# Layer 2 of a four-layer graph network by two tanh and a mask applied afterwards, and residual sums split over two engines

## What is computed

```
e     = leaky(einsum('bid,bjd->bij', x * a0, x))     # slope 0.2
alpha = sigmoid(where(adj == 1, e, -3.4e38))         # 0 where there is no edge
out   = alpha @ x + bias
```

## Time and profile before

| | us |
|---|---|
| median of 3 runs | 270.03 (268.92 to 270.17) |
| span of the profiled execution, first to last instruction | 268.6 |
| VectorE busy in it | 247.2 (92%) |
| TensorE busy (matmul) | 237.0 (88%) |
| ScalarE busy | 217.9 (81%) |
| GpSimd busy | 139.0 (52%) |

### The profile page before, as it was taken

How to read it: one execution, slowest core, us unless ns; L and a number is a source line. 1 busy time by engine, 2 the same in 40 slices (tenths; PEclk the granted TensorE clock), 3 DMA queues, 4 the chain that set the end, 5 groups by cost and what they waited for, 6 DMA issues and landing times.

```text
span 268.6 us, 6069 instructions
## 1 busy us (share of the span) xinstructions
PE 237.0 (88%) x1825; PEld 210.1 (78%) x1825; DVE 247.2 (92%) x956; ACT 217.9 (81%) x626; POOL 139.0 (52%) x161
## 2 busy tenths in 40 slices
PE   7887969889998999999999899999999959996850
PEld 7765768678886989888898788988999859785740
DVE  1598998999999989999999999999999999999883
ACT  1366525688899999899899999999999979977841
POOL 1001102511384485689647717554598457778851
PEclk9999988999999999999999999999999999999985
DMA  6597371000070003506000633103000110100033
GB/s 237 193 307 264 118 248 67 1 2 0 2 263 13 2 0 115 202 14 221 1 5 0 198 114 122 41 1 121 0 2 0 41 41 7 36 0 1 4 117 122
DMA packets 12147, 21.79 MB, mean 81 GB/s; under 512 B 1104, under 2 KB 5968, under 8 KB 12112
## 3 DMA queue, kind: packets, MB, share of 16 engines
q1 hardware_dynamic: 11680, 21.17, 22.9%
q10 hardware_dynamic: 432, 0.20, 0.3%
HBM read 17.17 MB, written 4.19 MB: 80 GB/s over the span
## 4 chain that ended last, share of the span: by engine, by line
DVE 49%; PE 28%; issue 8%; POOL 6%; ACT 5%; DMA 2%; DVEq 0%; POOLq 0%; ACTq 0%
PE banks L1123 13%; DVE wgt_all L808 10%; DVE fstats L856 8%; DVE fres L849 7%; DVE fres L841 5%; POOL frstd L542 4%; DVE wgt_all L815 3%; PE banks L1089 3%; DVE raw_all L731 3%; PE banks L1064 2%; PE banks L1120 2%; PE banks L1133 2%; DMA adj_all<-adj_turned 2%; PE banks L1081 1%; PE banks L1049 1%
## 5 line engine op out<-in xcount | busy, mean ns | idle before, releaser
L542 POOL TENSOR_TENSOR frstd<-fvar,minus_half 128x4 f32<-128x4 f32 x64 | 74.2, 1165 | 104.7 <-DVE fvar L862 36.6
L1123 PE MATMUL banks<-vals_all,wgt_all 128*128 128x129 f32 x512 | 64.4, 279 | 3.1 <-DVE wgt_all L808 2.9
L1123 PEld LDWEIGHTS banks<-vals_all,wgt_all 128*128 128x128 f32 x512 | 60.6, 194 | 4.8 <-issue 3.2
L808 DVE SCALAR_TENSOR_TENSOR wgt_all<-banks,gain,maskT 128x256 f32<-128x256 f32 x128 | 52.6, 473 | 0.6 <-PE banks L1081 0.3
L538 POOL TENSOR_TENSOR xb<-xs_all,bias_cen 128x256 f32<-128x256 f32 x60 | 44.1, 760 | 8.6 <-DVE xs_all L765 4.4
L856 DVE BATCH_NORM_STATS2 fstats<-fres 128x6 f32<-128x256 f32 x128 | 47.8, 416 | 0.0
L1089 PE MATMUL banks<-fxT,fxTa 128*128 128x256 f32 x128 | 35.8, 382 | 0.0
L1123 PE MATMUL banks<-xs_all,wgt_all 128*128 128x128 f32 x256 | 31.6, 277 | 4.8 <-DVE wgt_all L815 4.7
L1123 PEld LDWEIGHTS banks<-xs_all,wgt_all 128*128 128x128 f32 x256 | 29.9, 192 | 5.4 <-issue 3.2
L640 ACT ACTIVATE xs_all<-fres,frstd 128x128 f32<-128x128 f32 x96 | 30.9, 425 | 1.9 <-POOL frstd L542 1.8
L578 ACT COPY fxT<-banks 128x256 f32<-128x256 f32 x64 | 21.1, 396 | 10.9 <-PE banks L1049 10.8
(11 more groups left out here) (95 smaller groups left out, 463.1 us busy)
## 6 DMA issues: line engine op xcount, KB each, us to landing
adj_all<-adj_turned SPq DMA_DIRECT2D x16, 512.0 KB, 4.8
xT_all<-x_turned SPq DMA_DIRECT2D x16, 256.0 KB, 4.7
x_all<-x_laid SPq DMA_DIRECT2D x16, 256.0 KB, 4.4
out<-xs_all SPq DMA_DIRECT2D x16, 256.0 KB, 2.4
bias<-biases_laid SPq DMA_DIRECT2D x1, 128.0 KB, 3.6
w_pack<-W_and_columns ACTq DMA_DIRECT2D x1, 68.0 KB, 2.6
w_fast<-W_turned ACTq DMA_DIRECT2D x1, 64.0 KB, 4.1
w_nat<-in_L_gnn_W ACTq DMA_DIRECT2D x1, 64.0 KB, 4.4
```

Of the source, the lines that this page charges most:

```text
L542: nc.gpsimd.tensor_tensor(frstd[:, int(l), slot(n), :], fvar[:, int(l), slot(n), :], minus_half[:, :, :], ALU.pow).then_inc(fast_pool[k], 1)
L808: last = nc.vector.scalar_tensor_tensor(out=wgt(u)[:, c, :], in0=place(f"rows{l}", u), scalar=gain[:, u, c, 1:2], in1=maskT(u)[:, c, :], o ...
L1123: last = nc.tensor.matmul(place(f"out{l}", u)[:, b * width:(b + 1) * width], wgt(u)[:, c, b * P:(b + 1) * P], (vals if l in "01" else xs)( ...
```

## The change

1. `score` has no second product: L1090, `minus_big`, `raw` and its ring go. ScalarE takes `Tanh` of half the score and of a tenth of it; VectorE takes the larger as before (now called `umax`, into `sg`), and a new second pass (`alpha`) makes (tanh + 1) times the mask. The mask holds 0.5 instead of 1, so that this is the sigmoid. Layer 3's weights are doubled once to make up for it (one VectorE instruction), and `seen` reads the masks.
2. `res2` of teams 0 to 13 and `res3` of teams 0 to 10 become two steps: `lift`, a ScalarE copy from PSUM to `fres`, and a GpSimd addition in SBUF. Teams 14 and 15 of `res2` and 11 to 15 of `res3` stay on VectorE.
3. Small steps change engine: `var` of 16 team-layers and one `fscale` go from VectorE to GpSimd; `norm2` is on ScalarE for all 16 teams (5 were on VectorE), `norm3` for 15 (13), `norm1` for 14 (16); one `mask` and one `high` go to VectorE, and VectorE has two `bias2` and two `bias3` where it had two `bias3`.
4. All five orders and the bank table are new. Rings: `ADJ` 4 (3), `MASK` 10 (9), `SG` 4 (3), `RAW` gone. In SP's order the loads of teams 12 to 15 are now interleaved with the stores of teams 0 to 4.

The diff, cut to its core:

```
-X_IN, XT_IN, ADJ, RAW, MASK, XS, FXT, FXTA, VALS, WGT, SG, FRES, XB = 4, 3, 3, 7, 9, 6, 7, 5, 6, 7, 3, 9, 5
+X_IN, XT_IN, ADJ, MASK, XS, FXT, FXTA, VALS, WGT, SG, FRES, XB = 4, 3, 4, 10, 6, 7, 5, 6, 7, 4, 9, 5
+EDGE = 0.5
...
# order of ScalarE, end
+        "sigmoid:15 norm2:13 high:13 agg:12 norm3:11 agg:13 norm2:14 high:14 norm2:15 high:15 agg:14 norm3:12 agg:15 "
+        "norm3:13 norm3:14 norm3:15"
...
# order of VectorE, end
+        "bias2:14 norm1:15 bias2:15 res3:11 stats3:11 stats2:13 var3:11 var2:13 norm3:10 umax:14 alpha:14 umax:15 "
+        "alpha:15 res2:14 stats2:14 var2:14 res2:15 stats2:15 var2:15 res3:12 stats3:12 res3:13 stats3:13 var3:12 "
+        "var3:13 bias3:15 low:15 res3:14 stats3:14 res3:15 stats3:15 var3:15"
...
# GpSimd
+            def residual(l, n, k):
+                for u in graphs(n):
+                    biaser = doer(f"bias{l}", n)
+                    pool.wait_ge(signals[biaser][k], at(biaser, f"bias{l}", u))
+                    pool.wait_ge(fast_act[k], at("act", f"lift{l}", u))
+                    nc.gpsimd.tensor_tensor(fres(u)[:, :, :], fres(u)[:, :, :], xb(u)[:, :, :], ALU.add).then_inc(fast_pool[k], 1)
+            def variances(l, n, k):
+                pool.wait_ge(fast_dve[k], at("dve", f"stats{l}", final(n)))
...
+                nc.gpsimd.tensor_scalar(var, squares, factor, floor, ALU.mult, ALU.add).then_inc(fast_pool[k], 1)
...
# ScalarE
-                    nc.scalar.copy(maskT(u)[:, :, :], adj_in(u)[:, :, :]).then_inc(fast_act[k], 1)
+                    nc.scalar.activation(maskT(u)[:, :, :], adj_in(u)[:, :, :], ACT.Copy, scale=EDGE).then_inc(fast_act[k], 1)
...
-                    nc.scalar.activation(sg(u), scored, ACT.Sigmoid)
-                    nc.scalar.activation(wgt(u), scored, ACT.Sigmoid, scale=SLOPE).then_inc(fast_act[k], 1)
+                    nc.scalar.activation(sg(u), scored, ACT.Tanh, scale=0.5)
+                    nc.scalar.activation(wgt(u), scored, ACT.Tanh, scale=0.5 * SLOPE).then_inc(fast_act[k], 1)
+            def lift(l, n, k):
+                act.wait_ge(fast_pe[k], at("pe", f"out{l}", final(n)))
+                for u in graphs(n):
+                    nc.scalar.copy(fres(u)[:, :, :], place(f"out{l}", u).rearrange("p (b c) -> p b c", b=NB)).then_inc(fast_act[k], 1)
...
# VectorE
-                    nc.vector.tensor_scalar(raw(u), adj_in(u)[:, :, :], -1.0, 1.0, ALU.mult, ALU.add).then_inc(fast_dve[k], 1)
...
+            def larger(l, n, k):
+                for u in graphs(n):
+                    dve.wait_ge(fast_act[k], at("act", "sigmoid", u))
+                    nc.vector.tensor_tensor(sg(u), sg(u), wgt(u), ALU.max).then_inc(fast_dve[k], 1)
             def alpha(l, n, k):
-                    nc.vector.tensor_tensor(wgt(u), sg(u), wgt(u), ALU.max).then_inc(fast_dve[k], 1)
+                    nc.vector.scalar_tensor_tensor(out=wgt(u), in0=sg(u), scalar=1.0, in1=maskT(u), op0=ALU.add, op1=ALU.mult).then_inc(fast_dve[k], 1)
...
# TensorE
-                        nc.tensor.matmul(place("score", u)[:, c * N:(c + 1) * N], fxTa(u)[:, c * P:(c + 1) * P], fxT(u)[:, :], start=True, stop=False)
-                        last = nc.tensor.matmul(place("score", u)[:, c * N:(c + 1) * N], minus_big[:, :], raw(u)[:, c, :], start=False, stop=True)
+                        last = nc.tensor.matmul(place("score", u)[:, c * N:(c + 1) * N], fxTa(u)[:, c * P:(c + 1) * P], fxT(u)[:, :], start=True, stop=True)
...
+            def emptied_by(phase, n):
+                lifted = doer(f"res{phase[-1]}", n) == "pool"
+                return (fast_act, "act", f"lift{phase[-1]}") if lifted else (fast_dve, "dve", f"res{phase[-1]}")
```

114 lines of the change are left out of this document (69 added, 45 removed), and 196 rows, old and new, of tables (BANKS, ORDER).

## The result

The changed kernel takes 282.61 us, the median of 4 runs (279.82 to 284.27), and the kernel before 270.10 in 4 runs beside it; the ratio is 1.043, with a 95% interval of 1.034 to 1.053. Some executions of a kernel are over 1.5% slower than its fastest; ratios and intervals in this document leave them out, medians and ranges keep them. The changed kernel is slower by 12.5 us where the forecast had it faster by 5.

What follows compares the result with a forecast made beforehand. VectorE was taken as the bound, with ScalarE and TensorE also full in the middle. Span 268.6 - 8.8 - 2.5 + 3.5 + 2.6 = 263.4 us, plus 1.4 gives 264.8 us; range 258 to 271.5.

Steps and rivals of the forecast that it cites:

- the work counted out: VectorE's instructions removed, moved and added, summed part by part: -8.8 us, between -10.7 and -4.9.
- the term of the shared resource: GpSimd's additions and VectorE passes slow each other by waiting: +3.5 us, bounds 0 and 26.
- GpSimd's queue: On GpSimd, `pow` queues behind additions that wait for their lifts, delaying `norm` and `center1`; costed at nothing.
- The price of the new pass: VectorE's new `alpha` pass in layer 2: 0.66 us each, +21.1 us, bounds +19.2 and +25.0.
- 10.6 us for `raw`: VectorE's `raw` passes go, 0.66 us a team over 16 teams: -10.6 us.
- 16.5 for the sums: 25 residual sums leave VectorE, 0.66 us each: -16.5 us.
- the ends: Start and end of the kernel; the last team's `norm2` and `norm3` move to ScalarE: +2.6 us, bounds 0 and +5.
- TensorE's relief: 64 products, 17.4 us busy, leave TensorE; half of VectorE's idle time between 20 and 201 us credited: -2.5 us.
- Rival 4: ScalarE's table loads stay, so its middle work grows: 281.8 us, chance 0.04.
- rival 2: ScalarE becomes the bound of the middle through lifts and normalizations: 269.5 us, chance 0.13.
- rival 3: The saving comes whole; additions meet nothing new and moved normalizations hide: 258.7 us, chance 0.18.
- Rival 1: The lock between VectorE passes with two SBUF inputs and GpSimd additions costs more than gained: 273.4 us, chance 0.13.

Runs made afterwards that it cites:

- e8: The changed kernel without layer 2's new second VectorE pass (mask and +1 left out): 265.4 us, ratio 0.986.
- e12: The kernel before without `raw`, the mask added as 512 by the second product and offset by the sigmoid's bias, `dmax` in PSUM: 270.8 us, ratio 1.010.
- e15: e12 with Tanh in place of Sigmoid (the +1 left out): 268.5 us, ratio 0.998 to the kernel before.
- e16: e15 with the 64 mask products also left out, so layer 2 is not masked: 269.7 us, ratio 0.999 to the kernel before.
- e17: e12 (with Sigmoid) with the 64 mask products left out, so layer 2 is not masked: 270.6 us, ratio 1.001 to the kernel before.
- e1: The kernel before with only layer 2's new formula, all residual sums on VectorE, old orders, banks and rings: 289.5 us, ratio 1.068.
- e2: The changed kernel with all residual sums of layers 2 and 3 back on VectorE, no lifts: 282.9 us, ratio 1.045 to the kernel before.
- e3: The changed kernel with GpSimd's 50 residual sums cut to one column of 128: 268.3 us, ratio 0.998 to the kernel before.
- e5: The changed kernel with the second tanh kept in PSUM, so `umax` and `alpha` read one SBUF operand each, banks handed out anew: 275.5 us, ratio 1.022.
- e5b: Control for e5: the changed kernel with only its PSUM banks handed out anew: 283.0 us, ratio 1.051 to the kernel before.
- e11: The kernel before without the second score product (layer 2 not masked, `raw` still made): 272.0 us, ratio 1.004.
- e4: The kernel before with Tanh in place of Sigmoid and nothing else (the +1 left out): 272.7 us, ratio 1.012.
- e14: e12 with `norm2` of nine teams moved from ScalarE to VectorE: 278.9 us, ratio 1.035 to the kernel before.
- e10: The kernel before with `dmax` in PSUM alone, so `shift` has one SBUF input: 270.5 us, ratio 0.988.
- e13: e12's mask by an offset with Sigmoid, in the new orders with split sums, the larger taken in PSUM, banks new: 301.3 us, ratio 1.117.

## Why the prediction was wrong

**The sum, term by term.** The forecast had a span of 263.4 us: VectorE busy 247.2 - 8.8 + 3.5 = 241.9, and idle 21.4 - 2.5 + 2.6 = 21.5. Measured are 248.8 and 33.6. Of the 19.0 us missed 12.1 are idle time, and 7.8 are waits inside VectorE's instructions (11.3 for the term of 3.5); the work counted out was 0.9 better than forecast. So two steps failed: the term of the shared resource was mis-sized, and idle time was carried over from the kernel before, with GpSimd's queue and the new place of the second pass put at nothing.

**The price of the new pass was right, what was set against it was not.** The forecast set 10.6 us for `raw` and 16.5 for the sums against +21.1 for `alpha`. Where nothing meets it, `alpha` takes (255.41 - 254.21)/2 = 0.60 us from one start to the next, the lower bound of the forecast's 0.66, and 0.82 in the mean with its waits; left out alone it gives 17 us (e8). `raw` gave nothing: in e12, e15, e16 and e17 it is gone and nothing is in its place, and none is faster than before. In those four ScalarE's longer instructions in layer 2, 6 us, may have eaten part of a gain. e1 has none of that and agrees: 19.5 us for a net of 10.5 in work, so that `raw` gave at most 1.6 unless the pass costs more than its own 21.1. `raw` depended on nothing but a load and filled VectorE while the other engines' results were on their way, so that VectorE was busy 65.7 of 67 us and yet had this much to spare; the new pass stands between the sigmoid and the product with x, where every team waits for it. This reading of the two places is argued from the runs; measured is that the time stays when `raw` goes, and that the pass is 17 us (e8), and 19.5 with `raw` gone (e1).

**The sums' 16.5 us were given back.** The term for the shared resource, +3.5 with bounds 0 and 26, is the one that was mis-sized: VectorE's lost time grew by 21.9 - 10.6 = 11.3 us. e2 (12.3 with the sums back), e3 (10.8 with them short) and e5 (13.6 with one operand in PSUM) each take it away by another road, and e5 against e5b shows the mechanism, as only where operands lie, and the banks with it, was changed. I scaled by the number of additions from a trace in which pairs rarely met; 50 more additions and 32 more passes that read two SBUF tensors meet far more often. The Trainium skill (SBUF — State Buffer, Who interferes with whom) describes this exclusive use by an instruction of VectorE with two SBUF inputs against one of GpSimd that reads SBUF; the trace agrees, 6.38 us for a `pow` pair beside such passes and 2.00 without.

Busy VectorE by the prediction's own terms: 247.2 - 8.8 + 11.3 = 249.7 against 248.8 measured; so the work counted out was right within 1 us (with the pass at the 0.60 that it takes, 247.8).

**Idle time had next to no term.** The sum kept VectorE's 21.4 us but for -2.5 and the ends. Measured are 33.6, so 12.2 us more: 7.2 of it after 250 us, where the prediction had +2.6 for normalizations moved to ScalarE, 3.6 between 20 and 250, the rest in the start. The queue on GpSimd, costed at nothing but the lock, is the step I had named as the one that failed if idle exceeds 26, and it did. The runs give it a part only: with the sums back idle is 27.2 (e2), so some 4 to 6 us belong to the way over ScalarE and GpSimd. The other 6 to 8 are there without the split sums, and e1 has 9.0 more than before in the old orders, so the new pass in place of `raw` can bring as much. e5, with GpSimd's lost time at 4.5 us and idle still at 32.4, doesn't settle more, because of its banks. What the new orders alone would have was not run.

**TensorE's relief** was credited 2.5 us for 17.4 us of products gone. It is worth nothing (e11, e16, e17). TensorE is busy 238.9 us where 219.6 was forecast, and here the reading itself was wrong: 17.4 us is the length of 64 records that overlap their neighbours, while I had taken VectorE's work from one start to the next. By that count the products are 7.0 us. What lies between the 230.0 that this gives and 238.9 is not explained; the longer time at the lower clock lengthens records and may be part of it.

**ScalarE and GpSimd** came as forecast: one table load (18 before), ScalarE 212.5 (215), GpSimd 187.3 (173 to 185, plus its lost time). Rival 4 falls by the one load, rival 2 by ScalarE's 58.77 of 67 us in the middle, rival 3 by the sign. The Trainium skill (ScalarE: Activation LUTs, Table sets) puts tanh and exp into one set, and the trace agrees. The same page adds a drain of 1380 ns to a load (What ACT_TABLE_LOAD costs). It is not seen here: 17 loads less took 21.2 us off ScalarE's busy time in e4, 1.25 each, no more than the 1283 ns that one load takes, and in the earlier trace rows neither side of a load has a gap of more than 0.03 us.

**Rival 1**, the lock, with 273.4 us and a chance of 0.13, named the right mechanism on the right side. It stopped 9 us short: its 12.1 us of waits are what came (11.3), but it set them against a gain of 8.7 that was mostly not there, and had no term for idle time.

**The common fault** is that one engine's work was turned into time one for one because that engine was 92% busy. It held or fell short for work added (e1, e14, and the new pass in e8), and failed for work removed beside it (e11, e12, e15 to e17, and e4 for ScalarE).

What stays open: how much of the idle time belongs to the new orders alone; how much ScalarE's longer instructions hide in e12 and e15 to e17; what a bank held longer costs by itself; and whether orders planned anew for one pass in layer 2 (e12's formula, e10's operands) would turn 10 us less work into time. None of these was tried.

## What to carry to other kernels

Before an operation is moved to GpSimd, count not only its own time but the VectorE instructions with two SBUF inputs that it will meet, down to those of four elements a partition; where one of two inputs can stay in PSUM without holding a bank longer, try that first (it freed `shift` from its delays in e10; a gain in time was not shown). In a kernel whose orders are fixed by hand, work that waits for nothing can be filler: taking it out gave nothing here, while a pass put between two engines cost most of its length. Read what a matmul costs from one start to the next, not from its group's busy time. Try an edit in the old orders before you add its microseconds up.

## What the runs showed of the hardware

- Small instructions pay as much as large ones: a `shift` of 8 columns took up to 718 ns before and 714 after over a median of 157 and 160, and 164 at most with one operand in PSUM (e10).
- Of the instructions with one SBUF tensor as input, `var` (L911, 4 columns) was lengthened too: a median of 170 ns and up to 687 in the changed kernel. The 128 `weight` passes of 256 columns, which read one operand from PSUM, and the 128 statistics, with one input, lost nothing.
- A `pow` of 4 columns on GpSimd takes 1.02 us (median), and took 5.39 beside VectorE passes back to back.
- A pass over 512 columns costs the same from PSUM as from SBUF when nothing meets it (676 to 688 ns mean in e5, 682 median in the changed kernel).
- `Tanh` and the exponential, mixed in the new orders, need 1 load in all; `Sigmoid` and the exponential in the same orders took 28 loads, 36 us of ScalarE (e13).
- A bf16 matmul of 256 columns between two fp32 ones has a record of 0.273 us and takes 0.109 from its start to the next one's (kernel before).
- A `Sigmoid` over 512 columns takes 0.602 us, and 0.698 with a bias read per partition (e12).
